# One launch of a two-layer model: in the first attention the selection's sums and the row mask go to ScalarE, the weighing moves a slot later, and the inner norm's scale and shift are folded into the FiLM weights

## The reference, cut to what matters

```python
Q = (x_text @ Wq).reshape(Bb, Tt, H, DH)            # H = 4 heads of 32
K = (x_vision @ Wk).reshape(Bb, Gg, H, DH)
scores = einsum('bthd,bghd->bhtg', Q, K) / sqrt(DH)  # masked by vision_mask
topv, topi = top_k(scores, 32);  probs = softmax(topv)
attn = zeros_like(scores).at[..., topi].set(probs)
attn_mean = attn.mean(axis=1)
c_t = einsum('btg,bgd->btd', attn_mean, x_vision @ Wv) * text_mask
x = layernorm(x_text, g_norm_in, b_norm_in)
scale_in, shift_in = split(c_t @ W_film_in + b_film_in)
x = x * (1.0 + mod_gate * scale_in) + mod_gate * shift_in
y = s4d(x, ...)                                      # convolution over positions
```

## Time and profile before

| what | value |
|---|---|
| time, median of 3 runs | 1040.04 us (1036.32 to 1053.82) |
| span of the profiled execution | 1025.8 us |
| its own time | not given apart; median less span is 14.2 us |
| mean granted clock | 0.810 |
| busy PE / DVE / ACT / POOL | 741.2 / 685.5 / 456.1 / 575.1 us |

### The profile page before, as it was taken

The page is one execution under the profiler, slowest core; times in us unless marked ns, Lnnn a source line. Parts: engine busy times, 40 slices in busy tenths (PEclk is TensorE's granted clock), DMA queues, the critical chain, the costliest instruction groups (busy, mean ns, idle before and its releaser), DMA issues. The chain is left out here.

```text
span 1025.8 us, 21613 instructions
## 1 busy us (share of the span) xinstructions
PE 741.2 (72%) x6690; PEld 525.1 (51%) x6690; DVE 685.5 (67%) x3220; ACT 456.1 (44%) x1217; POOL 575.1 (56%) x944
## 2 busy tenths in 40 slices
PE   0687889796749999429892279989898756877750
PEld 0344445453736565225561157766666535777650
DVE  6998899887236876761110848977878564777754
ACT  3656665554004554202231747755556214544430
POOL 6788888868355442026663744455655452556550
PEclk9867887867559999768996559988988667999985
DMA  6300114994129785013542300000000016766517
GB/s 130 69 7 9 40 52 87 98 82 59 41 120 288 246 251 161 11 12 67 87 116 74 112 1 4 8 23 21 25 19 24 25 39 200 220 191 203 160 36 246
DMA packets 98690, 93.94 MB, mean 92 GB/s; under 512 B 37497, under 2 KB 82288, under 8 KB 98001
## 3 DMA queue, kind: packets, MB, share of 16 engines
q1 hardware_dynamic: 91126, 78.82, 31.1%
q0 software_dynamic: 6592, 13.58, 5.2%
q10 hardware_dynamic: 858, 0.17, 0.1%
HBM read 47.24 MB, written 43.19 MB: 88 GB/s over the span
## 5 line engine op out<-in xcount | busy, mean ns | idle before, releaser
L2342 POOL DMA_INDIRECT expert_pairs<-e_ys,e_home x78 | 78.9, 1011 | 76.5 <-DVE e_ys L2364 58.1
L1766 POOL DMA_INDIRECT expert_slots<-r_rows,r_slotu x64 | 63.2, 988 | 47.8 <-DVE r_rows L2095 31.7
L1750 POOL TENSOR_SCALAR a_kb<-a_kr,a_m,a_bk 128x128 f32<-128x128 f32 x128 | 57.5, 449 | 49.5 <-ACT a_kr L1963 32.9
L918 DVE MATCH_REPLACE8 work<-m,work 128x64 f32<-128x64 f32 x384 | 75.6, 205 | 0.0
L2309 PE MATMUL e_ps<-e_XH,e_wh 128*128 128x256 f32 x156 | 49.1, 315 | 26.7 <-DVE e_hh L2376 23.4
L1948 ACT ACTIVATE a_pp<-a_dd 128x512 f32<-128x512 f32 x64 | 40.2, 629 | 59.7 <-DVE a_dd L2135 57.2
L1537 POOL DMA_INDIRECT ex_rows<-rows,slot_source x32 | 30.7, 961 | 53.3 <-POOLq L1215 43.9
L905 DVE MAX8 m<-work 128x8 f32<-128x64 f32 x384 | 56.9, 207 | 0.0
L793 PE MATMUL psf<-filmw,us 97*128 97x512 f32 x64 | 51.3, 897 | 1.1 <-ACT FO L814 1.0
L2174 DVE RECIPROCAL a_rt<-a_pso 128x128 f32<-128x128 f32 x31 | 29.5, 953 | 30.7 <-PE a_pso L1876 21.3
L1591 ACT ACTIVATE ex_hs<-ex_psh,vec 128x512 f32<-128x512 f32 x32 | 20.9, 687 | 65.4 <-remote 36.2
(11 more groups left out here) (443 smaller groups left out, 2388.1 us busy)
## 6 DMA issues: line engine op xcount, KB each, us to landing
expert_slots<-rt_unfilled SPq DMA_DIRECT2D x151, 130.0 KB, 2.9
e_wf<-folded_weights SPq DMA_DIRECT2D x39, 386.0 KB
e_xr<-expert_slots SPq DMA_DIRECT2D x39, 130.0 KB
planes<-rt_zeros SPq DMA_DIRECT2D x4, 1024.0 KB
ew<-in_L_ffn_ew SPq DMA_DIRECT2D x16, 256.0 KB
comb_y<-planes SPq DMA_DIRECT2D x16, 256.0 KB, 5.7
pair_y<-expert_pairs SPq DMA_DIRECT2D x16, 256.0 KB, 5.8
folded_weights<-fold_done SPq DMA_DIRECT2D x8, 384.0 KB, 4.1
```

What stands on the lines that cost most here:

```text
L918: return own.did(dve.match_replace(wk_[x.j][:, h, :], m8[x.j][:, h, r, :], src[:, h, :], TAKEN))
L1750: m = pool.tensor_scalar(kb[a.j][:, :, h, :], k, m4[:, h:h + 1], bk4[:, h:h + 1], ALU.mult, ALU.add)
L1766: pool.indirect_dma_start(G.slots, bass.IndirectOffsetOnAxis(ap=slot[:, b, k, t:t + 1], axis=0), rb[b % NB][:, k, t, :], None).then_inc(se ...
L2342: pool.indirect_dma_start(G.pair, bass.IndirectOffsetOnAxis(ap=home[i % NY][:, k:k + 1], axis=0), ys[i % NY][:, k, :], None).then_inc(kept ...
```

## The change

Four things are changed, all in the first attention.

1. VectorE no longer sums the masked exponentials or multiplies by the row mask. ScalarE sums, by four copies with an accumulated output (one per head, 128x64, their copy thrown into `ee`), and after VectorE's reciprocal it multiplies the inverse by the row mask (`rs[:, 2, :]`). VectorE's reciprocal moves behind the third `max` of the slot.
2. GpSimd weighs tile x - 2 in slot x, where it weighed x - 1, and writes to a new pair `pw`. All that follows it (turning `at`, `abd`, `u`, `us`, FiLM, `XM`) moves one slot later, and each loop gets one slot more.
3. `gin` and `bin` are folded once into `filmw` (`fold_norm`, slot 1, three instructions on GpSimd); two of the five instructions of each `XM` go.
4. SP's code is as before.

```diff
                 def slot(x):
-                    j, a, c, m, n = x.j, x.by(3), x.by(-4), x.by(-1), x.by(1)
+                    j, a, c, w, n = x.j, x.by(3), x.by(-5), x.by(-2), x.by(1)
+                    if x.t == 1:
+                        fold_norm()
...
-                        step.then(pool.tensor_tensor(xn[:], xn[:], G.gin[:], ALU.mult))
-                        step.then(pool.tensor_tensor(xn[:], xn[:], G.bin[:], ALU.add))
...
-                    turn, qk, score, attn, vec, film = (x.by(d) for d in (3, 2, 1, -1, -2, -3))
+                    turn, qk, score, attn, vec, film = (x.by(d) for d in (3, 2, 1, -2, -3, -4))
...
+                    if p.real():
+                        act.wait_ge(s["masked"], p.t + 1)
+                        after(act, s["attn"], p.t - 1)
+                        for h in range(H0):
+                            m = act.activation(ee[p.j][:, h, :], pr[p.j][:, h, :], ACT.Copy, accum_out=rs[p.j][:, 0, h:h + 1])
+                        m.then_inc(s["summed"], 1)
...
+                    if p.real():
+                        if p.t == 0:
+                            act.wait_ge(s["side_kept"], made("mask"))
+                        act.wait_ge(s["inverse"], p.t + 1)
+                        act.activation(rs[p.j][:, 2, :], rs[p.j][:, 1, :], ACT.Copy, scale=G.tmask[:, p.t:p.t + 1]).then_inc(s["weights"], 1)
...
-                    if p.real():
-                        own.wait(masked)
-                        summed = own.did(dve.tensor_reduce(rs[p.j][:, 0, :], pr[p.j][:], AX.X, ALU.add))
...
+                def invert(p):
+                    if p.real():
+                        dve.wait_ge(s["summed"], p.t + 1)
+                        dve.reciprocal(rs[p.j][:, 1, :], rs[p.j][:, 0, :]).then_inc(s["inverse"], 1)
```

More of the change, by code:

```diff
@@ L578, in first_attention @@
         dd, ee, pr = two("dd", [P, H0, T]), two("ee", [P, H0, T]), two("pr", [P, H0, T])
-        rs, at, abd = two("rs", [P, 2, H0]), G.at0["at"], G.at0["abd"]
+        rs, at, abd = two("rs", [P, 3, H0]), G.at0["at"], G.at0["abd"]
+        pw = two("pw", [P, H0, T])
         us, fi = G.at0["us"], two("fi", [P, 256])
@@ L592, in first_attention @@
             "ctx_kept", "weights", "dve", "pool", "toeplitz", "normal", "gated", "film_rows",
-            "side", "side_kept", "powers", "power", "factors", "kernel", "kernel_rows")}
+            "masked", "summed", "inverse", "film_folded", "side", "side_kept", "powers", "power", "factors", "kernel", "kernel_rows")}
         fold, K = G.fold, G.kernel
@@ L697, in kernel_part, with fold_norm @@
                         pool.tensor_tensor(K.K, K.K, K.skip, ALU.add).then_inc(s["kernel"], 1)
+                def fold_norm():
+                    gain, moved = G.filmw[:, 0:D], G.filmw[:, D:2 * D]
+                    pool.wait_ge(s["side_kept"], made("film"))
+                    step.then(pool.tensor_tensor(xn[0:DC + 1, :], gain, G.bin[0:DC + 1, :], ALU.mult))
+                    step.did(pool.tensor_tensor(moved, moved, xn[0:DC + 1, :], ALU.add))
+                    step.then(pool.tensor_tensor(gain, gain, G.gin[0:DC + 1, :], ALU.mult))
+                    pool.sem_inc(s["film_folded"], 1)
                 def slot(x):
-                    j, a, c, m, n = x.j, x.by(3), x.by(-4), x.by(-1), x.by(1)
+                    j, a, c, w, n = x.j, x.by(3), x.by(-5), x.by(-2), x.by(1)
+                    if x.t == 1:
+                        fold_norm()
                     if x.real() and x.t % 8 == 0:
@@ L711, in slot @@
                         pool.wait_ge(s["scores_sb"], n.t + 1)
[L712 to L717, removed]
+                    if w.real():
+                        pool.wait_ge(s["weights"], w.t + 1)
+                        step.then(pool.tensor_tensor(pw[w.j][:], pr[w.j][:], wide(rs[w.j][:, 2, :].unsqueeze(2), [P, H0, T]), ALU.mult))
+                        after(pool, s["attn_turned"], w.t - 1)
+                        step.did(pool.tensor_tensor(pw[w.j][:, 0:2, :], pw[w.j][:, 0:2, :], pw[w.j][:, 2:4, :], ALU.add))
                         step.wait()
-                        pool.tensor_tensor(at[m.j][:, 0:T], pr[m.j][:, 0, :], pr[m.j][:, 1, :], ALU.add).then_inc(s["attn"], 1)
+                        pool.tensor_tensor(at[w.j][:, 0:T], pw[w.j][:, 0, :], pw[w.j][:, 1, :], ALU.add).then_inc(s["attn"], 1)
                     if a.real():
@@ L732, in slot @@
                     kernel_part(x.t)
-                march(slot, -3, NT + 4)
+                march(slot, -3, NT + 5)
             @block.tensor
@@ L807, in slot @@
                         pe.transpose(psb[attn.j][:, 0:P], at[attn.j][:], G.ident[:]).then_inc(s["attn_turned"], 1)
-                march(slot, -3, NT + 3)
+                march(slot, -3, NT + 4)
             @block.scalar
@@ L843, in slot @@
                 def slot(x):
-                    turn, qk, attn, vec, film, score, n = (x.by(d) for d in (3, 2, -1, -2, -3, 1, KEPT))
+                    turn, qk, attn, vec, film, score, n, p = (x.by(d) for d in (3, 2, -2, -3, -4, 1, KEPT, -1))
                     if score.real():
@@ L930, in slot @@
                         found = top(x, 0, sc[j], None)
-                    if p.real():
-                        own.wait(masked)
-                        summed = own.did(dve.tensor_reduce(rs[p.j][:, 0, :], pr[p.j][:], AX.X, ALU.add))
[L934 to L947, removed]
+                        done = [replace(x, 0, sc[j], h, found) for h in range(H0)]
                         for r in range(1, KTOP // 8):
                             found = top(x, r, wk_[j], done)
+                            if r == 2:
+                                invert(p)
                             done = [replace(x, r, wk_[j], h, found) for h in range(H0)]
                         last[t] = done[-1]
+                    else:
+                        invert(p)
+                def invert(p):
+                    if p.real():
+                        dve.wait_ge(s["summed"], p.t + 1)
+                        dve.reciprocal(rs[p.j][:, 1, :], rs[p.j][:, 0, :]).then_inc(s["inverse"], 1)
                 march(slot, 0, NT + 1)
```

9 lines of the change are left out of this document (4 added, 5 removed).

## The result

The changed kernel takes 1059.67 us (median of 4 runs, 1054.67 to 1067.49) against 1038.18 (median of 4, 1030.11 to 1053.82): ratio 1.0227, 95% interval 1.0169 to 1.0285. It is slower by about 21.5 us. The ratios leave out slow executions, here before's 1053.82, so they are not the quotients of the medians. The profiled execution took 1067.49 us with a span of 1066.3, so its own time lies above the median by 7.8 us.

A forecast was written before the change was run, and what follows sets the result against it. VectorE looked like the bound, GpSimd in slots 4 to 10. Slots 1 to 11 -5.3, 12 to 29 +11.7, 30 and 31 -0.9, drain -2.1: together +3.4 us, span 1029, time 1044; range 1014 to 1066.

The forecast's parts named there:

- dear sums together with the stalls: Upper end of the range: costly accumulated sums on ScalarE plus the store stalls, 1066 us.
- The forecast's own range, 1028 to 1056: Range of the main forecast, stalls of about 3.8 us that eat the gain; chance 0.52.
- The 14.2 us that it put on the span: Amount by which before's median was taken to lie above its traced span of 1025.8 us.
- Part 5, the new wait: ScalarE's "first" copy waits for the late `fold_done` store: six stalls of 3.8 us, slots 12 to 27, 22.8 us.
- The clock, 1 us a cycle: Slots 12 to 29: TensorE's low clock adds 1 us to each three-slot cycle, 6.0 us in all.
- The third rival: TensorE's clock falls after every stall; "second", scores and FiLM run at half clock: +13, 1057 us; chance 0.16.
- Part 4, cycles of 18.1 us: Slots 12 to 29: three slots take 5.7, 5.7 and 6.7 us, 18.1, or 17.0 without `XT`.
- Part 3, sums at 1.4 us: ScalarE's four accumulated sums cost 1.4 us a slot, between 0.5 and 2.2; the mask's factor 0.2.
- The second rival: ScalarE is the bound: sums at 2.2 us make its slot 6.5 us, 1064 us; chance 0.15.
- Part 2, GpSimd as the bound in slots 4 to 10: Two instructions removed save GpSimd 1.06 us a slot; six slots there go from 46.40 to 40.0 us.
- Slots 30 and 31, and the drain: Slots 30 and 31 take 11.4 against 12.3 us; the drain, a last-tile chain, 11.1 against 13.26.
- The first rival: The store is no bound on ScalarE: sum of -22, or -30 with cheap sums, 1010 to 1020 us; chance 0.17.

The follow-up runs named there:

- two buffers: The changed kernel with two alternating buffers for the folded weights `fold_done`, SP's order unchanged: 975.5 us, beside 972.52 for before.
- SP in step: The changed kernel with SP loading the context tile one place nearer (RING - 3 for RING - 2): 1043.61 us, ratio 0.9989 to before.
- the filler: The changed kernel with 12 unread transposes on TensorE ahead of each "second" piece from slot 6 on: 983.12 us, ratio 1.0175 to before.
- filler in step: The changed kernel with SP's context load one place nearer and 4 unread transposes behind most side pieces: 1039.12 us, ratio 1.0029 to before.
- the fold alone: The kernel before with only `fold_norm` added and two instructions a slot taken off GpSimd: 1030.13 us, ratio 0.9842 to before.

## Why the prediction was right in kind and too small in size

1059.67 lies in the range of 1014 to 1066, and part of that is luck: the upper end was set by dear sums together with the stalls, and the sums were not dear. The forecast's own range, 1028 to 1056, was missed. The forecast was +3.4 us on before, and 1044 is 5.8 above the median now measured; the measured difference is 21.5. The 14.2 us that it put on the span had its source in before's trace, which is of a quick execution; in each execution timed here span and time differ by 1.2. By its steps, with slots 12 to 29 counted in cycles of three:

- **Part 5, the new wait: right.** Six stalls in the six slots named. They are 18.1 us, 3.0 each, where 22.8 stood in the sum: five of the stores landed 2.9 to 3.2 us after their issue, not 4.1; the sixth took 6.9, but had gone out early. The experiments show its cause from both sides: added to before it costs 27.3 us, taken from after it gives 31.4 (two buffers) and 29.8 (SP in step).
- **The clock, 1 us a cycle: the term that was mis-sized.** Slots 12 to 29 less the stalls are 138.4 us, where the prediction's pace of 106.4 and its 6.0 for the clock make 112.4. Of the 26 missing, 13.3 (31.4 - 18.1) vanish with the stalls; the filler puts the clock's share at 11 us of the 31.4 or more. The third rival, clock falling after every stall, was the nearer case, in the sum (1057) and in kind, but it counted "second", the scores and FiLM only. It left out that the next "first" can run at half clock too, 5.7 us instead of 3.5, as in two cycles here.
- **Part 4, cycles of 18.1 us: too short by 2.1.** The other 12.7 stay with two buffers: 125.09, 20.8 a cycle. I had ScalarE's 1 us at `abd` in each "first", and had not seen that sums and reciprocal stand behind `abd`. A late "first" now stops VectorE in mid-round (20.2 us in 12 waits, SP in step), where in before the sum was VectorE's own. Moving the reciprocal only renamed the wait. At a clock of 0.94 the cycle is 18.6 us (filler in step, slots 14 to 22), so much of the 2.1 goes with the clock even without stalls; what would hold a whole stretch there stays open.
- **Part 3, sums at 1.4 us: a little too dear.** They are four steps of 0.24, 1.0 us; the factor is 0.30, not 0.2. The second rival, ScalarE as the bound by dear sums, falls.
- **Part 2, GpSimd as the bound in slots 4 to 10: wrong.** Slots 1 to 11 did gain 6.9 where 5.3 stood in the sum, but by another cause: the fold alone gives 0.4. The six slots of GpSimd's that took it 46.40 us took VectorE 42.45 (58.47 to 100.92), so GpSimd fell behind, and the stretch did not run at its pace. Relieved, it waits for VectorE instead (the row below, of the fold alone in slots 1 to 11), and that the sum came out near is luck. The gain came with the sums leaving VectorE: 74.45 with them there, 66.31 to 69.22 without, both with the fold. No run moves the sums without the fold. In the changed kernel those six slots of GpSimd's take 38.73 us without a gap and VectorE's 37.69; 1.06 a slot more would make them 45.1, an estimate, so the sums may need the fold for their gain.

```profile
POOL dd L716 <- DVE m L913: 8.8, 8, 2.6
```

- **Slots 30 and 31, and the drain: wrong.** 13.67 for 11.4, since the pair still lies in the low clock, and 13.84 for 11.1. I made the drain one chain of the last tile. It is four FiLM products in a row, at 276.92, 280.39, 283.86 and 287.33, each in a round of TensorE and ScalarE of 3.47 us at clock 0.50; and the last factor stands behind `abd` in ScalarE's queue. Two rows of TensorE, one of ScalarE:

```profile
276.92 2.05 PE L802 MATMUL psf<-filmw,us 97*128 97x512 f32 x2 [0.75 <-ACT FO L823]
...
280.39 2.05 PE L802 MATMUL psf<-filmw,us 97*128 97x512 f32 x2 [0.69 <-ACT FO L823]
```

```profile
280.60 0.30 ACT L902 ACTIVATE rs<-rs,tmask 128x4 f32<-128x4 f32 x1
```

The fold alone, without the extra slot in the pipeline, drains in 10.50: there the drain gives what was forecast.

The first rival, the store as no bound, at 1010 to 1020, would have been wrong also in its price: with no stall at all the kernel is at 0.9989 of before, not at 0.98.

## What to carry to other kernels

When a tile's work moves a slot later, every gate that counts that work moves with it, also on queues that the change doesn't edit: look for each wait on its semaphores, and for what is queued behind it. An idle stretch on TensorE is paid twice, once as the wait and once as half clock in the pieces behind it; price the second from the piece that runs next, not from the mean clock of a long stretch. Before an engine that shows no gaps is called the bound, take work off it alone: 4.4 us less of GpSimd in slots 1 to 11 gave 0.4. And read a stretch that a filler should quicken slot by slot: a mean clock of 0.81 held two slots at 0.55 and nine at 0.94.

## What the runs showed of the hardware

**A sum by ScalarE is two rows.** The grouped lines of the changed kernel, slots 1 to drain, by shape (busy us, mean ns; then idle before):

```profile
L867 ACT ACTIVATE ee<-pr 128x64 f32<-128x64 f32 x128 | 30.8, 248 | 1.6 <-DVE pr L946 1.6
L867 ACT ACTIVATION_READ_ACCUMULATOR ee<-pr 128x1 f32 x128 | 24.8, 193 | 0.0
```

Added up they would be 0.44 us, but the pairs start 0.24 us apart: most of the read is hidden. By the Trainium skill ("ScalarE: Activation LUTs", What ACT_TABLE_LOAD costs) an ACTIVATE of 64 elements with immediate operands is 239 ns, an estimate from the page's figures; the trace has 248. The page has no price for the read.

**A tiny VectorE instruction took over three times its time beside GpSimd.** Before's mask factor, 128 x 4 elements, in slots 1 to 4 (minimum, median and maximum in ns), and in all later ones:

```profile
L945 DVE TENSOR_TENSOR rs<-rs,tmask x4: 520/582/585, 40.6 to 60.3; 128x4 f32<-128x4 f32 x4
```

```profile
L945 DVE TENSOR_TENSOR rs<-rs,tmask x27: 143/161/680, 67.0 to 245.9; 128x4 f32<-128x4 f32 x27
```

The timeline of one of those that took 0.58 us:

```profile
46.98 0.73 POOL L709 TENSOR_TENSOR sc<-dd,pen 128x256 f32<-128x256 f32 x1
...
47.14 0.58 DVE L945 TENSOR_TENSOR rs<-rs,tmask 128x4 f32<-128x4 f32 x1
```

It starts inside GpSimd's `sc` and ends with it, at 47.7. Slots 1 to 4 of before are 6.56 us each (26.24 in four), 0.41 over slot 30's 6.15, and 0.42 is what this instruction takes more than its usual 0.16; after the change, which has no such instruction on VectorE, they are 5.80 (23.20). The Trainium skill ("SBUF — State Buffer", Who interferes with whom) states that a VectorE instruction with two SBUF inputs contends with a GpSimd instruction that reads SBUF, that the shared ports are an exclusive lock, and that the order of issue decides which of the two blocks. These rows agree; no experiment here took the GpSimd instruction away.
